# Expert blocks woven into the last batch's attention: two stacks, a late home for a batch's rows, copied labels

## The reference, cut to what matters

```python
x = x + _L0_attn_ref(_layernorm(x), W_theta, W_phi, W_g)
# on the result, with y = layernorm(x):
h = rmsnorm(y, ln1_w); q, k, v = h @ wqkv.T ...          # rope on q and k
y = y + softmax(causal(q @ k.T / 4)) @ v @ wo.T
h = rmsnorm(y, ln2_w)
topw, topi = top_k(softmax(h @ gate_w.T), 2)              # weights made to sum to 1
for e in range(8):
    g = silu(h @ w1[e].T) * (h @ w3[e].T)                 # 512 wide
    out = out + (g @ w2[e].T) * wfull[:, e:e + 1]
x = x + y + out
```

## Time and profile before

| | before |
|---|---|
| median of 3 runs | 1236.21 us (1233.28 to 1239.84) |
| the profiled execution's own time | 1235.77 us |
| its span | 1234.1 us |
| TensorE busy | 1112.5 us (90%) |
| TensorE weight loads | 605.3 us (49%) |
| VectorE busy | 697.8 us (57%) |
| ScalarE busy | 538.5 us (44%) |
| GpSimd busy | 406.6 us (33%) |
| mean granted TensorE clock | 0.967 of 2.4 GHz |

### The profile page before, as it was taken

How to read it: one execution, slowest core, us unless ns; L and a number is a source line. 1 busy time by engine, 2 the same in 40 slices (tenths; PEclk the granted TensorE clock), 3 DMA queues, 4 the chain that set the end, 5 groups by cost and what they waited for, 6 DMA issues and landing times.

```text
span 1234.1 us, 18221 instructions
## 1 busy us (share of the span) xinstructions
PE 1112.5 (90%) x6132; PEld 605.3 (49%) x6132; DVE 697.8 (57%) x1412; ACT 538.5 (44%) x1091; POOL 406.6 (33%) x428
## 2 busy tenths in 40 slices
PE   3988998999999899998888987896989999999997
PEld 2754443335544344644334432464656666666664
DVE  3378786776567677788664782246333333333332
ACT  3435765666555667564656765231111211211121
POOL 2021432123116323117753228342733322222222
PEclk9998998999999999998998998998999999999999
DMA  5022122214011324012584712421333232222220
GB/s 165 1 81 85 54 71 60 60 57 130 4 44 50 108 65 124 1 42 73 159 262 134 237 30 91 122 61 27 104 59 57 48 48 47 43 43 40 45 39 9
DMA packets 75882, 91.82 MB, mean 74 GB/s; under 512 B 16464, under 2 KB 63696, under 8 KB 75792
## 3 DMA queue, kind: packets, MB, share of 16 engines
q1 hardware_dynamic: 61824, 71.94, 19.9%
q0 software_dynamic: 13968, 18.71, 8.5%
HBM read 50.90 MB, written 35.89 MB: 70 GB/s over the span
## 4 chain that ended last, share of the span: by engine, by line
PE 65%; POOL 8%; issue 7%; DVE 6%; DMA 5%; SPq 4%; ACT 4%; POOLq 0%; DVEq 0%; ACTq 0%
PE psum L1776 17%; PE psum L1791 9%; PE psum L1729 8%; PE psum L1716 6%; POOL routed L1015 4%; PE psum L1703 3%; PE psum L1698 3%; PE psum L1684 3%; ACT probs_mem L1115 3%; DVE mx L1544 3%; PE psum L1736 3%; PE psum L1783 2%; DMA recip_rows<-recips 2%; PE psum L1660 2%; PE psum L1638 2%
## 5 line engine op out<-in xcount | busy, mean ns | idle before, releaser
L1544 DVE TENSOR_REDUCE mx<-psum 128x1 f32<-128x640 f32 (+6 forms) x352 | 346.9, 1023 | 106.2 <-PE psum L1704 98.5
L1115 ACT ACTIVATE probs_mem<-psum 128x512 f32<-128x512 f32 (+1 forms) x608 | 309.0, 582 | 185.6 <-PE psum L1716 184.2
L1776 PE MATMUL psum<-w_mem,stack_mem 128*128 x568 | 269.7, 598 | 11.9 <-DVE stack_mem L1592 10.3
L1023 POOL DMA_INDIRECT out<-stack_mem x71 | 110.5, 1557 | 266.5 <-DVE stack_mem L1608 203.9
L1716 PE MATMUL psum<-stack_mem 98*128 98x512 bf16 (+3 forms) x768 | 180.6, 336 | 17.3 <-DMA stack_mem<-mneg_parts 9.0
L1137 ACT ACTIVATE stack_mem<-psum 128x512 f32<-128x512 f32 x71 | 42.5, 599 | 325.3 <-PE psum L1776 325.3
L981 POOL TENSOR_SCALAR_AFFINE_SELECT probs_mem<-probs_mem 128x512 f32<-128x512 f32 x128 | 81.6, 638 | 289.0 <-ACT probs_mem L1115 288.3
L1776 PEld LDWEIGHTS psum<-w_mem,stack_mem 128*128 128x128 f32 x568 | 102.9, 192 | 85.3 <-issue 81.7
L1791 PE MATMUL psum<-w_mem,stack_mem 128*128 x568 | 134.4, 379 | 0.8 <-ACT stack_mem L1142 0.8
L1703 PE MATMUL psum<-stack_mem 96*128 96x256 bf16 (+3 forms) x448 | 127.9, 316 | 4.7 <-DVE mx L1544 3.2
L1791 PEld LDWEIGHTS psum<-w_mem,stack_mem 128*128 128x128 f32 x568 | 107.5, 190 | 42.7 <-issue 31.6
(11 more groups left out here) (301 smaller groups left out, 1257.3 us busy)
## 6 DMA issues: line engine op xcount, KB each, us to landing
stack_mem<-routed SPq DMA_DIRECT2D x71, 129.0 KB, 2.0
w_mem<-in_w13T SPq DMA_DIRECT2D x16, 512.0 KB, 4.7
qk_parts<-w_mem SPq DMA_DIRECT2D x16, 384.0 KB, 2.6
stack_mem<-qk_parts SPq DMA_DIRECT2D x32, 192.0 KB, 3.1
stack_mem<-qk_parts SPq DMA_DIRECT2D x32, 128.0 KB, 2.7
attnT<-heads_out SPq DMA_DIRECT2D x128, 32.0 KB
recip_rows<-recips SPq DMA_DIRECT2D x32, 128.0 KB
w_mem<-in_w2T SPq DMA_DIRECT2D x8, 512.0 KB, 6.8
```

The lines of the kernel that those rows point to most:

```text
L1023: e.indirect_dma_start(out_rows, bass.IndirectOffsetOnAxis(ap=blocks[w % NBLK].bitcast(I32)[:, D:D + 1], axis=0), youts[w % NYOUT], None, ...
L1115: e.activation(probs[m % 2][:, hh:hh + n, q0:CH], grid(turn[step][0][:, 0:n * (CH - q0)], n), ACT.Exp, scale=float(HD) ** -0.5).then_inc(s ...
L1544: e.tensor_reduce(to, took, AX.X, ALU.max).then_inc(sem["max"], 1)
L1776: m = e.matmul(bk, blockT[w % 2][:, k], w13_s[:, k, bass.ds(offset[w] + half * FFN, FFN)], start=(k == 0), stop=(k == KD - 1))
```

## The change

It gives the last batch two stacks in place of three, so that the third is free for the experts when head group 11 (the last of batch 2) is scored. The rows of h of batch 3 go into the memory of stack 0 (`hrow_late`), free when head group 14 is scored. Blocks (now 4) and outputs (4) of the experts move into the second half of hrow, free after the scatters of group 0; transposed blocks, gated and gatedT into the third stack; silu has no tile of its own, tanh writes into gated. Row number and weight of each block are copied by POOL into a small tile of their own (`label`, 128x2, 8 of them); a fetch then waits for the transpose and the label copy of block w - 4. The route of group 1 is due 30 units later, the last group's scatters 50 later, and every part of an expert step behind its first has due time 0.

```diff
-NBLK, NYOUT = 7, 4
+NBLK, NYOUT, NLABEL = 4, 4, 8
+STACK_OF = [n % NSTACK if n < (NBATCH - 1) * NKV else (n - (NBATCH - 1) * NKV) % (NSTACK - 1) for n in range(len(HEAD_GROUPS))]
+USES = [STACK_OF[:n + 1].count(i) for n, i in enumerate(STACK_OF)]
+def stack_before(n):
+    return max((m for m in range(n) if STACK_OF[m] == STACK_OF[n]), default=None)
+TO_EXPERTS = HEAD_GROUPS[max(n for n, i in enumerate(STACK_OF) if i == NSTACK - 1)]
+TO_ROWS = HEAD_GROUPS[max(n for n, i in enumerate(STACK_OF) if i == 0)]
...
-            return attended + [scatter_steps(gi)[-1]] + [("down", b - NBLK)] * (b >= NBLK)
+            return through(*TO_EXPERTS) + [scatter_steps(gi)[-1]] + [("blockT", b - NBLK), ("label", b - NBLK)] * (b >= NBLK)
+        if stage == "label":
+            return [("fetch", b)] + [("down", b - NLABEL)] * (b >= NLABEL)
...
+        later = 30 * (gi == 1)
+        streams += [(spread_over(at + 12 + later, at + 30 + later, route(gi)), False), (iter([(LATER + 100 * (gi == LAST) if step[0] == "scatter" else at + 30, step) for step in sent(gi)]), False)]
...
-            pending[following].setdefault(step[0], []).append((end + LATENCY, due, step, i + 1))
+            pending[following].setdefault(step[0], []).append((end + LATENCY, min(due, 0.0) if due >= LATER else due, step, i + 1))
...
+        hrow_late = stack_mem[:, 0:TPB * RW].rearrange("p (t c) -> p t c", t=TPB)
+        def row_tile(b, j):
+            return hrow_late[:, j] if b == NBATCH - 1 else hrow[:, (b * TPB + j) % NROW]
...
-        (rb, rhT, rsl, rg, rgT, ry) = carve(stack_mem, [NBLK * RW, 2 * KD * P, 2 * FFN, 2 * FFN, 2 * FFN, NYOUT * D])
+        (rhT, rg, rgT) = carve(stack_mem[:, (NSTACK - 1) * stack_n // 2:], [2 * KD * P, 2 * FFN, 2 * FFN])
+        (rb, ry) = carve(hrow_mem[:, TPB * RW:], [NBLK * RW, NYOUT * D])
...
-                    q.wait_ge("score_mm", last["score"])
-                    q.wait_ge("max_mm", last["max"])
+                    stack_read(q, *TO_EXPERTS)
                     if w >= 6:
                         q.wait_ge(*slot("block_load", 6, w - 6))
                     if w >= NBLK:
                         q.wait_ge("blockT_mm", w - NBLK + 1)
-                        q.wait_ge("y", w - NBLK + 1)
-                        q.wait_ge("add_out", 16 * (w - NBLK + 1))
+                        q.wait_ge("label", w - NBLK + 1)
...
+                elif stage == "label":
+                    w, = at
+                    q.wait_ge(*slot("block_load", 6, w))
+                    q.wait_ge("add_out", 16 * (w - NLABEL + 1))
+                    q.wait_ge("y", w - NLABEL + 1)
+                    e.tensor_copy(labels[w % NLABEL].bitcast(I32), blocks[w % NBLK].bitcast(I32)[:, D:D + 2]).then_inc(sem["label"], 1)
...
-                    q.wait_ge("gated", 2 * (w - 1))
-                    e.activation(silus[w % 2], turn[step][0], ACT.Tanh, scale=0.5).then_inc(sem["tanh"], 1)
+                    q.wait_ge("gatedT_mm", w - 1)
+                    e.activation(gated[w % 2], turn[step][0], ACT.Tanh, scale=0.5).then_inc(sem["tanh"], 1)
```

More of the change, by code:

```diff
@@ L131 @@
 LANDING = {"load_x": 5.0, "split_store": 2.6, "stack": 3.5, "maxT": 1.9, "pack": 2.2, "recip_store": 2.0, "spread": 2.4, "base_store": 4.0,
-           "fill": 6.0, "carry": 5.0, "w13": 14.0, "w2": 14.0, "scatter": 2.5, "fetch": 3.0}
+           "fill": 6.0, "carry": 5.0, "w13": 14.0, "w2": 14.0, "scatter": 2.5, "fetch": 3.0, "down": 2.5}
 WORK_OF = {
@@ L436, in plan @@
                (iter([(LATER, ("w13", k, x)) for k in range(KD) for x in range(NE)]), False), (iter([(LATER, ("w2", x)) for x in range(NE)]), False),
-               (iter([(-1.0, ("carry", gi)) for gi in range(1, len(GROUPS))]), False), (iter([(0.0, ("ids2",))]), False),
-               (iter([(LATER + w, ("fetch", w)) for w in range(len(WORK))]), False), (iter(experts()), False)]
+               (iter([(-1.0, ("carry", gi)) for gi in range(1, len(GROUPS))]), False), (iter([(0.0, ("ids", g[0])) for g in GROUPS[1:]]), False),
+               (iter([(LATER + w, ("fetch", w)) for w in range(len(WORK))]), False),
+               (iter([(0.0, ("label", w)) for w in range(len(WORK))]), False), (iter(experts()), False)]
     for stage in ("recip", "recip_store", "spread", "norm"):
@@ L442, in plan @@
         at = (g[-1] + 1) * WHOLE
-        streams += [(spread_over(at + 12, at + 30, route(gi)), False), (iter([(LATER + 50 * (gi == LAST) if step[0] == "scatter" else at + 30, step) for step in sent(gi)]), False)]
+        later = 30 * (gi == 1)
+        streams += [(spread_over(at + 12 + later, at + 30 + later, route(gi)), False), (iter([(LATER + 100 * (gi == LAST) if step[0] == "scatter" else at + 30, step) for step in sent(gi)]), False)]
     for b in range(NBATCH):
@@ L536, in plan @@
             if step[0] == "score":
-                progress = due if step != attended[0] else NEVER
+                progress = due if step != through(NBATCH - 1, NKV - 1)[0] else NEVER
         else:
@@ L729, in mega_kernel @@
         names = ["load_eye", "load_latent", "load_wg", "load_wqkv", "load_rope", "load_tri", "load_ids", "load_ln2", "load_wo", "load_gate",
-                 "x_half0", "x_half1", "set", "ids2", "carry_load", *[f"stack{i}_{c}" for i in range(NSTACK) for c in range(QR)],
+                 "x_half0", "x_half1", "set", "ids", "carry_load", *[f"stack{i}_{c}" for i in range(NSTACK) for c in range(QR)],
                  "pair_mm", "xnT_mm", "gram_mm", "square_mm", "x1_mm", "hT_mm", "v_mm", "k_mm", "q1_mm", "q2_mm", "max_mm", "maxT_mm",
@@ L982, in _ @@
                                     channel_multiplier=-1).then_inc(sem["mask"], 1)
-                elif stage == "ids2":
-                    landed(q, "scatter", 6, scatters(0))
-                    e.tensor_copy(hrow_i[:, 0:NTILE - NROW, D], ids_s[:, NROW:NTILE]).then_inc(sem["ids2"], 1)
+                elif stage == "ids":
+                    b, = at
+                    if b == NBATCH - 1:
+                        stack_read(q, *TO_ROWS)
+                    else:
+                        landed(q, "scatter", 6, scatters(0))
+                    to = hrow_late if b == NBATCH - 1 else hrow[:, 0:TPB]
+                    e.tensor_copy(to.bitcast(I32)[:, :, D], ids_s[:, b * TPB:(b + 1) * TPB]).then_inc(sem["ids"], 1)
                 elif stage == "base":
@@ L1019, in _ @@
                     gi, _ = WORK[w]
+                    q.wait_ge("label", w + 1)
                     q.wait_ge("add_out", 16 * w)
@@ L1586, in _ @@
                         landed(q, "scatter", 6, nth["scatter", gi, 0, nt - 1])
-                    e.tensor_copy(hrow[:, t0 % NROW:t0 % NROW + nt, D + 1], places(gi)[1][s]).then_inc(sem["weight"], 1)
+                    to = hrow_late if gi == LAST else hrow[:, t0 % NROW:t0 % NROW + nt]
+                    e.tensor_copy(to[:, :, D + 1], places(gi)[1][s]).then_inc(sem["weight"], 1)
                 elif stage == "blockT":
@@ L1597, in _ @@
                         q.wait_ge("up_mm", nth[step])
-                        q.wait_ge("gatedT_mm", w - 1)
-                        e.scalar_tensor_tensor(gated[w % 2], silus[w % 2], 1.0, turn[step][0], ALU.add, ALU.mult).then_inc(sem["gated"], 1)
+                        e.scalar_tensor_tensor(gated[w % 2], gated[w % 2], 1.0, turn[step][0], ALU.add, ALU.mult).then_inc(sem["gated"], 1)
                     else:
@@ L1607, in _ @@
                     q.wait_ge("add_out", 16 * (w - NYOUT + 1))
-                    e.tensor_scalar(youts[w % NYOUT], turn[step][0][:, 0:D], blocks[w % NBLK][:, D + 1:D + 2], None, ALU.mult).then_inc(sem["y"], 1)
+                    q.wait_ge("label", w + 1)
+                    e.tensor_scalar(youts[w % NYOUT], turn[step][0][:, 0:D], labels[w % NLABEL][:, 1:2], None, ALU.mult).then_inc(sem["y"], 1)
         @block.tensor
```

83 lines of the change are left out of this document (42 added, 41 removed).

## The result

The kernel after the change took 1196.38 us (median of 4 runs, 1195.52 to 1198.04) beside 1238.03 us for the kernel before on the same chip (4 runs, 1233.28 to 1239.87): ratio 0.967, 95% interval 0.964 to 0.970. Its profiled execution has a span of 1194.7 us where before had 1234.1, 39.4 us less.

A forecast was written before the change was run, and what follows sets the result against it. TensorE, busy 90% of the span, was taken as the bound, with 38.5 us of stalls and clock loss recoverable. Terms -12 - 3 - 11 + 3 = -23 us from 1235.77 gave 1213 us, range 1199 to 1230.

The forecast's parts named there:

- Rival C: Nearly all idle time closed, 36 to 38.5 us, giving 1197 to 1200 us; VectorE relief alone cures 754; chance 0.14.
- the wait at 754 us: End of batch 3's attention: TensorE waits 4.7 us for negated maxima, then half clock to about 763 costs 4 us.
- expert steps first (due time 0): VectorE's last route chain: expert steps go first, ending TensorE's 10.3 us wait; 12 us of 12.9 gained.
- block freed by transpose and label: Expert fetches no longer wait for late adds behind scatters on POOL; 3 us gained, bounds 0 and 3.1.
- weave in the attention: Expert blocks fill 60% of 14.0 + 4 us lost at 710 to 777 us; 11 us gained, bounds 3 and 18.
- stalls from two stacks: Last batch: later stack loads for head groups 14 and 15 cost 3 us of new stalls, bounds 0 and 21.
- before the output projection: Wait for normalised attention, 2.8 us, plus 1.7 us clock loss: 4.5 us left in place, no gain counted.
- The bound of 38.5 us: All recoverable TensorE time between 710 and 900 us: attention, output projection, last batch's route and a fetch.
- first expert matmul: Expected at 700 to 725 us in place of 776.77, once the expert weights have landed.
- The later route of group 1: Route goes behind all maxima, its scatters leave the last masks; cures TensorE's waits of 4.7 and 3.6 us.
- The last route chain: On VectorE, stretched over about five expert blocks, ending some 10 us later, hidden by 29 blocks, 169 us.
- The label copies: On POOL, 71 copies of 128x2 taken at 0.21 us each, costing nothing on the path.

The follow-up runs named there:

- neither: Kernel after without due time 0 and without the weave (fetch waits for the last score): 1231.4 us, ratio 0.992 to the kernel before.
- no weave: Kernel after with each fetch waiting for the last score again, due time 0 kept: 1214.28 us, ratio 0.981; in an earlier group 1227.96 us, 0.980.

## Why the prediction was wrong

The direction, the places and most mechanisms were right; the terms were too small. Rival C, "nearly all is closed", with 0.14, comes nearest (1197 to 1200 forecast, 1196.4 measured), though not for its reason: VectorE's relief alone takes away the wait at 754 us but not the loss. Of the 39.4 us, by the sum's own steps:

| term | forecast | found | from |
|---|---|---|---|
| expert steps first (due time 0) | 12 | 12.9 in this trace; 11.9 by itself (without the weave) | the wait and its clock loss are gone; neither against no weave |
| block freed by transpose and label | 3 | 3.1 | wait gone |
| weave in the attention | 11 | 15.6, of it 12.0 the weave's own | loss 18.2 to 2.6; no weave against the kernel after, 14.6 to 2.6 |
| stalls from two stacks | -3 | 0 | no such wait in the kernel after |
| before the output projection | 0 | 2.5 | 4.5 to 2.0 |
| waits not in the list (1.6 ahead of the first block, 1.7 for a rank) | 0 | 3.3 | gone |
| remainder | 0 | 2.6 | 39.4 - 36.8 |

The found terms make 40.0, against 39.4. Of the 16.4 us that the sum was short no term makes up more than a third: 4.6 in the attention, 3.3 of waits not in the list, 3 for the stacks, the remainder of 2.6, 2.5 before the output projection and 1 in the first two rows (together 17.0). The 1.6 us lay inside the prediction's window of 710 to 777 us, so it was among its 14.0.

**The step that failed** is "I take 60%, 11 us" for the weave. The runs with and without the weave measure 17.2 us for it, 12.0 in the attention and 5.2 in the tail, where the sum expected nothing of it. In the attention 86% of the 18.2 us of loss went, not 60%; some 3 us of that came without the weave. The reason given for 60% was that a block has five hops over VectorE and ScalarE, in queues where a maximum may be in front, and that TensorE executes in the written order. The change gives all those hops due time 0, so the planner takes them ahead of maxima and route steps that are ready, and the step doesn't reckon with it. The timelines above show the difference: a copy within 0.9 us with due time 0, one after 16 to 18 us without. The run without it looks like what the 60% described: 3.5 blocks up in place of 6.5, and 9.0 of the 15.0 us of loss filled that the version with neither had. That this is 60% as well is luck, as the two traces come from different groups. With due time 0, 2.6 us are left.

**"I leave the 4.5 us in place"** failed in the same way: the run with due time 0 but no weave still loses 6.3 us in the tail, the kernel after of its group 1.1. With blocks enough under way, TensorE waits 2.0 us for the normalised attention, at full clock; before it had waited 2.8 and run a stretch of 7.1 us at 0.76. The clock loss needed no cure of its own: with the stretches of idle time gone, the granted clock stayed at 1.00 from 700 us on.

**The 3 us of stacks** didn't show in the whole change. The load for head group 15 was issued from 704.69 to 711.42 us, as worked out (705 to 712), and no score or maximum waited for it: in the kernel after, TensorE's waits from 700 to 791 us are of 1.1 us and less.

**The bound of 38.5 us** was 2.9 us short of the 41.4 us of loss from 700 to 900 us, since in the tail it took only the largest waits; a wait of 1.7 us for a rank was left out. And the first expert matmul was forecast for 700 to 725 us, counting on w2: but the projection up needs only w13, and its first half ran at 680.33, a transpose at 648.46. So there was weaving ahead of 700 us, where the sum had nothing. Whether it gained there isn't shown: the remainder of 2.6 us has 1.6 us less of loss ahead of 700 us under it, and in the last group that loss is 4.7 us more.

**The later route of group 1** was to cure two waits. The one for the negated maxima it did cure, with and without the weave (it is in no trace with the later route). But "its 23 scatters leave the place beside the last masks" was wrong: without the weave the waits for masks grew to 9.7 us, 11.0 with due time 0 in the kernel before, and 7.8 in the kernel after without the weave. Within the weave they are 0.5 us, as expert work fills them, and with the early route there the wait for the negated maxima is only 0.8 us. So the weave closes either hole, and the later route adds some 3 us in the attention.

**Right.** The last route chain ran from 860.48 to 890.99 us, woven with expert steps: 30.5 us in place of the 16.8 of the earlier trace rows, so 14 us longer where 10 were forecast, and no matmul waited for it. The heads were to be finished near 790: 791.02. The label copies were taken at 0.21 us, which is right: POOL is busy 14.5 us more than before, 0.20 for each of 71, and hidden, as argued. The profile's sum of 45.2 us for the group counts more (last section).

**What stays open.** That the order without due time 0 has no expert block between the last output of the heads and the output projection is read from the trace; which of the planner's choices leads to it wasn't tried. The 7.6 us of the rest are seen in traces alone. Whether the weave without due time 0 gains or loses a few us is open: the table's row comes from another group of runs, in which the kernel after had 7.3 us of loss in place of 3.7, and the whole times don't show the 8.5 us. And the cost of two stacks alone is known to 6 us only.

## What to carry to other kernels

When independent work is woven into a stretch, judge it by how many pieces of it can be in flight, not by each hole: its steps on the other engines must stand ahead of the host's, or a hole opens elsewhere (here 19.9 us where the stretch ends). A chain moved off one engine's wait takes what follows it along: the later route brought its scatters in front of masks. Price two edits that act on the same queue together; one brought 11.9 us alone, the other no gain that can be told, the pair 29.1 (all in loss). And add up all idle time of a stretch before its largest waits are taken as the most that can be won.

## What the runs showed of the hardware

A 128x2 copy on POOL is recorded at two durations: 0.18 to 0.21 us, or 0.75 to 0.82. POOL's group of the copies in the kernel after, then POOL's timeline around a long one and a short one:

```profile
L1057 POOL COPY labels<-hrow 128x2 int32<-128x2 int32 x71 | 45.2, 636 | 12.6 <-DMA hrow<-routed 12.5
```

```profile
1102.08 1.56 POOL L1065 DMA_INDIRECT out<-hrow,labels  x1 [4.06 <-DVE hrow L1651]
1103.06 0.78 POOL L1057 COPY labels<-hrow 128x2 int32<-128x2 int32 x1
```

```profile
798.65 0.98 POOL L1050 DMA_INDIRECT routed<-hrow,route_b  x1 [0.30 <-issue]
799.33 0.69 DVE L1645 TENSOR_TENSOR stack_mem<-psum,stack_mem 128x512 f32<-128x512 f32 x1 [0.70 <-PE psum L1819]
799.62 0.21 POOL L1057 COPY labels<-hrow 128x2 int32<-128x2 int32 x1
```

The long copy is recorded from 1103.06 to 1103.84 us, but the indirect add ahead of it on POOL ends at 1103.64. So it is the add's last 0.58 us and 0.20 us more. That holds for all 71: the 54 long copies begin 0.54 to 0.61 us before the end of an add and end 0.19 to 0.24 us after it, and none of the 17 short ones begins under an add. The two records overlap, and the sum of 45.2 us counts that time twice, while the busy time of the engine, which grew by 14.5 us, doesn't. What POOL does for the copy under the add isn't shown. VectorE's work beside them doesn't decide it: from 900 to 941 us eight copies beside L1645 alone are long, and the one at 799.62 us, with the same L1645 beside it, is short. L1645 reads one tile in SBUF and one in PSUM. The Trainium skill (SBUF — State Buffer, Who interferes with whom) says that an instruction of VectorE with at most one SBUF input, outside its two-port modes, doesn't contend with GpSimd. The trace agrees at 799.62 us, where the copy takes 0.21 us beside it.

The granted clock follows the holes. Before, 8 of 41.4 us of loss were clock; after, none; without due time 0, with single waits of 19.9 and 10.7 us, 4.7 us were; with the fetch waiting for the add, with one of 4.9 us, 2.2 us. Behind the wait of 2.0 us that is the longest in the kernel after from 700 us on, TensorE runs on at 1.00.
